# Sixteen-head attentions of a fused four-layer kernel: values and divisors from one product of 32 columns, with block transposes on VectorE and the multiplication on GpSimd

## Reference

```python
# L0 "cross": keys and values from a context of 96 features, with biases and an output projection
# L2 "masked": the same without biases and projection; masked queries attend evenly
attn = softmax(q @ k.T * 8 ** -0.5)      # per head, 128 x 128
out  = attn @ v                          # per head, 128 x 8
...
# L2 "self": causal, 16 query heads, 4 key heads; q and k rotated, then normed
out  = softmax(causal(q @ k.T / sqrt(8))) @ v
gate = sigmoid(out @ Wg + bg)
x    = x + (out * gate) @ Wo + bo
```

## Time and profile before

| | |
|---|---|
| median of 3 runs | 1946.26 us (1944.96 to 1949.05) |
| profiled execution, its own time | 1934.08 us |
| its span | 1932.3 us |
| PE busy | 1597.6 us, 83% of the span |
| DVE busy | 1342.6 us, 69% |
| ACT busy | 959.0 us, 50% |
| POOL busy | 824.1 us, 43% |
| cross phase, about | 15 to 293 us |
| masked phase, about | 800 to 1058 us |
| self phase, about | 1065 to 1415 us |

### The profile page before, as it was taken

The page is one execution under the profiler, slowest core; times in us unless marked ns, Lnnn a source line. Parts: engine busy times, 40 slices in busy tenths (PEclk is TensorE's granted clock), DMA queues, the critical chain, the costliest instruction groups (busy, mean ns, idle before and its releaser), DMA issues. The chain is left out here.

```text
span 1932.3 us, 43308 instructions
## 1 busy us (share of the span) xinstructions
PE 1597.6 (83%) x14686; PEld 1248.9 (65%) x14686; DVE 1342.6 (69%) x4056; ACT 959.0 (50%) x1953; POOL 824.1 (43%) x1300
## 2 busy tenths in 40 slices
PE   5999985977799989788997699999849699999840
PEld 3666664966577778565664466666639598888730
DVE  4878873348787777677775688888647488888522
ACT  2666662533333334366665477777725344444310
POOL 2334444346300000111111777799654555565426
PEclk9989997987799999699999699999969899999965
DMA  6657304821000000000000000000029100000043
GB/s 193 226 181 233 102 12 133 250 71 41 17 1 2 1 1 1 6 8 8 8 7 2 1 2 2 2 9 9 9 80 262 45 15 13 19 20 19 11 147 87
DMA packets 60807, 108.72 MB, mean 56 GB/s; under 512 B 11715, under 2 KB 49620, under 8 KB 59796
## 3 DMA queue, kind: packets, MB, share of 16 engines
q1 hardware_dynamic: 54452, 93.45, 15.6%
q0 software_dynamic: 6144, 12.60, 2.2%
HBM read 89.49 MB, written 52.17 MB: 73 GB/s over the span
## 5 line engine op out<-in xcount | busy, mean ns | idle before, releaser
L711 DVE TENSOR_REDUCE parts<-PS 128x8 fp32r<-128x1024 f32 x192 | 234.5, 1221 | 145.2 <-PE PS L457 145.0
L928 ACT ACTIVATE P<-PS 128x1024 f32<-128x1024 f32 x192 | 198.1, 1032 | 105.4 <-PE PS L472 105.2
L905 ACT CAST qS<-PS 32x512 fp32r<-32x512 f32 x384 | 220.8, 575 | 9.5 <-PE PS L424 6.1
L274 POOL TENSOR_TENSOR ve<-mv,eps_t 128x1 f32<-128x1 f32 x160 | 31.7, 198 | 403.9 <-DVE mv L270 403.5
L1757 DVE SCALAR_TENSOR_TENSOR X<-PS,wt,X 128x128 f32 (+1 forms) x480 | 134.9, 343 | 46.1 <-PE PS L1600 38.3
L1889 ACT ACTIVATE P<-PS,w_f_b 128x512 f32<-128x512 f32 x128 | 88.0, 687 | 142.4 <-PE PS L1581 140.9
L1600 PEld LDWEIGHTS PS<-w_f_w,P 128*128 128x128 f32 x1024 | 129.9, 193 | 39.7 <-issue 27.7
L1600 PE MATMUL PS<-w_f_w,P 128*128 128x128 f32 x1024 | 141.8, 282 | 13.6 <-DVE X L1757 11.8
L472 PE MATMUL PS<-qS,kS 128*128 128x512 f32 x384 | 151.8, 451 | 1.0 <-ACT P L928 1.0
L424 PE MATMUL PS<-ident_r,parts 128*128 128x128 f32 x768 | 124.3, 293 | 27.1 <-issue 26.2
L424 PEld LDWEIGHTS PS<-ident_r,parts 128*128 128x128 f32 x768 | 104.4, 201 | 45.7 <-issue 39.5
(11 more groups left out here) (301 smaller groups left out, 4329.6 us busy)
## 6 DMA issues: line engine op xcount, KB each, us to landing
P<-in_f_blob SPq DMA_DIRECT2D x12, 578.0 KB, 4.8
Y<-in_f_blob SPq DMA_DIRECT2D x11, 578.0 KB, 5.1
ctxT<-in_ctxT SPq DMA_DIRECT2D x128, 48.0 KB, 1.8
tok<-hs SPq DMA_DIRECT2D x46, 128.0 KB, 3.5
hs<-yo SPq DMA_DIRECT2D x46, 128.0 KB, 4.2
P<-in_f_blob SPq DMA_DIRECT2D x12, 450.0 KB, 4.4
Y<-in_f_blob SPq DMA_DIRECT2D x11, 450.0 KB, 4.5
w_f_w<-in_f_w SPq DMA_DIRECT2D x2, 1024.0 KB, 5.7
```

What stands on the lines that cost most here:

```text
L711: e.tensor_reduce(parts[:, it.s, 0, 8 * half:8 * half + 8, 3, 0], S_ps[:, :, :].rearrange("p i (j t) -> p (i j) t", t=T), AXX, ALU.max)\
L905: m = e.copy(qS[r, it.s % 2, :, j, :], TP[0][r, :].rearrange("p (g t) -> p g t", g=4))
L928: e.activation(P[:, it.s % 2, 8 * half:8 * half + 8, :].rearrange("p h t -> p (h t)"), ST_ps[:, :, :].rearrange("p j n -> p (j n)"), ACT.E ...
```

## The change

The sums come out of the product with `vx` itself. Each block of 32 columns of `vx` has 16 columns that are zero when only two heads are added up. So a call of `pe_values` is now for a pair of heads of each group: pair 0 writes values to rows 0 to 15 of each block and the sums to rows 16 and 17; pair 1 writes values to rows 16 to 31 and sums to rows 0 and 1. Columns of ones (`sum_cols`) stand in `vx` for that; `ones_x` and its 16 matmuls per item are gone. A sum is now in a row of its own, while the values that it divides are in other rows, so DVE first turns the bank `OB[:, 0:256]` in squares of 32 x 32 into SBUF (`oV`, tokens by features), takes the reciprocal of 16 sums per row, and the product `oN` is then made with a broadcast along the row, in two instructions of 64 columns: in cross and masked on POOL, in self on DVE. A second instruction of DVE, `v_heads_back`, turns `oN` back to `oT`; in cross and masked it stands at the end of DVE's tick, behind the second `v_max`.

```diff
             def pe_values(e, it, pair):
...
-                        e.wait_ge(s_o, at(s_o, it.n))
-                for j in range(4):
+                        e.wait_ge(s_tv, at(s_tv, it.n))
+                for j in (2 * pair, 2 * pair + 1):
                     for g in range(4):
...
+                        m = e.matmul(OB[32 * g:32 * g + 32, pair * T:(pair + 1) * T],
+                                     vx[:, it.s, 128 * j + 32 * g:128 * j + 32 * g + 32],
+                                     P[:, it.s % 2, 4 * g + j, :], start=(j % 2 == 0), stop=(j % 2 == 1))
...
             def v_heads(e, it):
+                e.wait_ge(s_av, at(s_av, it.n + 1))
+                if due(2 * it.n):
+                    e.wait_ge(s_on, at(s_on, 2 * it.n))
+                e.transpose(oV[:, :, :, :].rearrange("p a q r -> p (a q r)"), OB[:, 0:2 * T]).then_inc(s_tv, 1)
+                e.wait_ge(s_tv, at(s_tv, it.n + 1))
+                e.reciprocal(rec[:, :, :, :], sums).then_inc(s_rec, 1)
+                if causal:
+                    normed(e, it)
+
+            def normed(e, it):
...
+                e.wait_ge(s_rec, at(s_rec, it.n + 1))
+                for pair in range(2):
+                    own_rows = slice(16 * pair, 16 * pair + 16)
+                    e.tensor_tensor(oN[:, :, own_rows].rearrange("p q (h d) -> p q h d", h=2),
+                                    oV[:, pair, :, own_rows].rearrange("p q (h d) -> p q h d", h=2),
+                                    rec[:, pair].unsqueeze(3).broadcast_to([T, 4, 2, DH]), ALU.mult).then_inc(s_on, 1)
+
+            def v_heads_back(e, it):
...
-                e.wait_ge(s_rec, at(s_rec, it.n + 1))
-                e.tensor_tensor(oT[:, it.s, :], OB[:, 0:T], rec[:, :], ALU.mult).then_inc(s_o, 1)
+                e.wait_ge(s_on, at(s_on, 2 * it.n + 2))
+                e.transpose(oT[:, it.s, :], oN[:, :, :].rearrange("p q r -> p (q r)")).then_inc(s_o, 1)
...
                             v_residual(e, it)
                         if it := item(L):
                             v_max(e, it, 1)
+                        if it := item(L + 3):
+                            v_heads_back(e, it)
...
                     if it := item(F + 1):
                         g_low(e, it)
+                    if it := item(L + 3):
+                        normed(e, it)
```

More of the change, by code:

```diff
@@ L209, in build @@
         vx = sb("vx", [T, RING, 4 * 136])
-        ones_x = sb("ones_x", [T, 4, 4, DH])
+        sum_cols = [vx[:, :, 128 * j:128 * j + 128].rearrange("p r (g c) -> p r g c", c=32)
+                    [:, :, :, (16, 17, 0, 1)[j]:(16, 17, 0, 1)[j] + 1] for j in range(4)]
         qT = sb("qT", [D, RING, T], F32R)
@@ L475, in pe_scoresT, with pe_values @@
                 m.then_inc(s_st, 1)
-            def pe_values(e, it, what):
-                if what == 0:
+            def pe_values(e, it, pair):
+                if pair == 0:
                     issued["av"] += 1
@@ L484, in pe_values @@
                     if due(it.n):
-                        e.wait_ge(s_o, at(s_o, it.n))
-                for j in range(4):
+                        e.wait_ge(s_tv, at(s_tv, it.n))
+                for j in (2 * pair, 2 * pair + 1):
                     for g in range(4):
[L488 to L492, removed]
+                        m = e.matmul(OB[32 * g:32 * g + 32, pair * T:(pair + 1) * T],
+                                     vx[:, it.s, 128 * j + 32 * g:128 * j + 32 * g + 32],
+                                     P[:, it.s % 2, 4 * g + j, :], start=(j % 2 == 0), stop=(j % 2 == 1))
+                if pair == 1:
                     m.then_inc(s_av, 1)
@@ L871, in pool @@
                     return
-                for item in unrolled(last if post else F + 1):
+                for item in unrolled(last if post else L + 3):
                     if it := item(0):
@@ L979, in attention16 @@
                    hi=B, lo=2 * B, turn=B, kx=B, qT=B, tk=B, kS=B, tq=B, qS=B, s=2 * B, mx=2 * B,
-                   st=2 * B, exp=2 * B, av=B, rec=B, o=B, out=B, done=B, pad=n_pad)
+                   st=2 * B, exp=2 * B, av=B, rec=B, values_turned=B, values_normed=2 * B, o=B, out=B, done=B,
+                   pad=n_pad)
             if projected and not causal:
@@ L1114, in pool @@
                 e.memset(vx[:], 0.0).then_inc(sem("pad"), 1)
+                e.wait_ge(sem("pad"), at(sem("pad"), 1))
+                for j in range(4):
+                    e.memset(sum_cols[j], 1.0).then_inc(sem("pad"), 1)
                 if pre:
@@ L1151, in attention1 @@
             totals(stats=B, rstd=B, h=B, bn=B, ve=B, hps=B, hT=B, qkv=B, qk=2 * B, v=B, s=B, mx=B, nb=B,
-                   exp=B, pps=B, pT=B, av=B, rec=B, done=B, pad=1)
+                   exp=B, pps=B, pT=B, av=B, rec=B, done=B, pad=5)
             totals(**{f"ctx{i}": 16 * GROUPS for i in range(RING)})
@@ L1357, in v_heads @@
                     ob = OB[:, :].rearrange("p (h n) -> p h n", n=T)
-                    e.reciprocal(rec[:, 0:4].unsqueeze(2), ob[:, :, HD:HD + 1]).then_inc(s_rec, 1)
+                    e.reciprocal(rec8[:, :].unsqueeze(2), ob[:, :, HD:HD + 1]).then_inc(s_rec, 1)
                     if half == 0:
```

22 lines of the change are left out of this document (13 added, 9 removed).

## The result

The changed kernel took 1931.38 us in the median of 20 runs (1893.92 to 1961.69); the kernel before, on the same chips, 1941.79 (1933.79 to 1951.87). The ratio is 0.9844, interval 0.9812 to 0.9876. Over all runs the medians give 1931.38 / 1941.79 = 0.9946, and resampling the recorded runs puts that between 0.989 and 0.997. So it is faster either way, by a half to one and a half per cent. The number in microseconds is the forecast one (1931); the gain by the ratio, 1.56%, is twice the forecast 0.8%, and the one by the medians, 0.54%, less than it. And the spread is new: 68 us for 18.

A forecast was written before the change was run, and what follows sets the result against it. No engine is always busy; closed chains of engines set each tick. Masked -11.4, cross -11.6, self +5, clock +4, rest -1 sum to -15 us, taking the median from 1946.3 to 1931 us; range 1912 to 1952.

The forecast's parts named there:

- masked, mechanics: Masked: DVE's shorter heads and PE's earlier values cut the tick by 0.38 to 7.17 us; 30 ticks, -11.4 us.
- cross, mechanics: Cross: DVE's saving goes into waiting for POOL, PE turns `h` sooner; 0.40 us over 29 ticks, -11.6 us.
- self: Self: new DVE and POOL work lengthens the tick by 0.15 us over 31 ticks, +5 us.
- clock, cross and masked: Cross and masked: PE idles longer ahead of `h`, so three more drops from 2.4 to 1.2 GHz, +4 us.
- what would make it wrong: Sign against the forecast: a clock at 1.2 GHz for whole ticks.
- the clock falls twice as often: Rival, cross and masked: 14 more drops at 1.47 us, +21 for +4, 1948 us, no change; 10%.
- the chain of DVE and POOL: Self: five new instructions add 0.35 us, making this chain the longer one, 10.47 for 10.22 us.
- rival of self: Two: DVE held up beside POOL's work, +16 us, 1947, 12%; or ACT and PE set the tick, 1916, 10%.
- Unit prices: Assumed times of the new instructions: first transpose 0.45 us, transpose back 0.32, reciprocal 0.25, POOL's products 0.62 for two.
- The rival of two passes: DVE's transposes take two passes, 0.22 and 0.10 us more per item; +7 us, 1953 us, slower; 12%.

The follow-up runs named there:

- before_filled_at_scores: Kernel before with two unused 128 x 128 products ahead of the second half of the scores in cross and masked; 1930.71 us, ratio 0.9964.
- fill_behind_pair_0: Changed kernel with 8 extra matmuls per item behind pair 0 in all three phases, into columns nobody reads; 1898.34 us, ratio 0.9768.
- fill_not_in_self: Changed kernel with 8 extra matmuls behind pair 0 in cross and masked, but not in self; 1892.9 us, ratio 0.9772.
- the doubled transpose: Changed kernel with 8 extra matmuls behind pair 0 and the first transpose made twice in all phases; 1926.59 us, ratio 0.9931.
- before_filled: Kernel before with 8 more matmuls per item behind the first call of the product, into columns nobody reads; 1974.28 us, ratio 1.0197.
- fill_ahead_of_scores: Changed kernel with two unused 128 x 128 products ahead of the second half of the scores in cross and masked; 1917.55 us, ratio 0.988.
- the load back: Changed kernel with 8 unused matmuls behind each call of the value products, 32 matmuls per item as before; 1901.4 us, ratio 0.979.
- fill_product_on_vector: Changed kernel with 8 extra matmuls behind pair 0 and the product on DVE right behind the reciprocal; 1947.21 us, ratio 1.0039.

## Why the prediction was right in its number, and where it failed

Three kernels that are nearly always at 2.4 GHz in cross and masked separate the terms: before_filled_at_scores for the kernel before, fill_behind_pair_0 and fill_not_in_self for the changed one. Their ticks at 2.4 GHz are those of the unfilled kernels (7.55 and 6.97 in masked), so what the unfilled ones are longer by is the clock's.

| term, us | forecast | measured |
|---|---|---|
| masked, mechanics | -11.4 | -17 to -18 (228.9 to 210.5-211.7) |
| cross, mechanics | -11.6 | -14 to -16 (237.3 to 221.4-223.3) |
| self | +5 | +1.6 (301.6 to 303.2) |
| clock, cross and masked | +4 | +24 to +36 (below) |

- **The clock** is the step that failed: "so I allow three more drops: +4 us". The kernel before lost 245.6 + 238.0 - 237.3 - 228.9 = 17 us to it. The changed one lost 41 to 45 us in one profile (244.4 + 232.0 against 431.9 to 435.0) and 51 to 54 in the other: 24 to 36 more. These are single profiles, and that of the kernel before is of an execution near its fastest (1934.08 us, median 1941.79), so its 17 us are rather low. The runs give a check: the filled kernels differ by 0.9772 / 0.9964 = 0.981, some 37 us, and the unfilled by 10 in the medians, so the change lost some 27 us more. The form was wrong as well as the size. I read the falls of before as single events and counted more of them; in the long stretches at 2.4 GHz there are none now, and a fall, when it comes, lasts for whole ticks, which the prediction named only as what would make it wrong. The rival "the clock falls twice as often" had the right sign and neither form nor price.
- **Masked** was mis-sized: 6.97 for a forecast 7.17 and 7.55 before. Heads came to 0.63 for 0.72, maximum to `kx` to 4.01 for 4.17, `kx` to the end of `h` to 1.56 for 1.60. The rest, `h` to PE in 0.06 and PE's 1.34 to the next maximum, was as forecast.
- **Cross** too: -0.45 to -0.51 us per tick for -0.40, of which 0.05 may be the one fall that the 237.3 still hold. The transpose back waits 0.27 us in the row shown, inside the forecast 0.2 to 0.3, and 9.0 us in 26 cases on the whole. That `kx` starts hardly earlier held (3.00 for 3.10, and 3.08 before), and what is left is PE's, as reasoned.
- **Self** lost 0.05 us per tick and not 0.15. DVE waited 5 times for POOL's power, 4.5 us in all (2 times before, 3.1 us), where the prediction had it in most ticks: the chain of DVE and POOL, lengthened by 0.35 in the sum, did not become the one that sets the tick, which went from some 10.2 to 10.26 us; the doubled transpose shows that a third of such work counts. L657 ran 0.317 to 0.592 us as before, so nothing more is held up, and neither rival of self came.
- **Unit prices**: first transpose 0.42 (0.45), second 0.311 (0.32), reciprocal 0.25 (0.25), POOL's product 0.294 (0.31). The rival of two passes is excluded. The Trainium skill's 311 ns for a 128x128 transpose (VectorE: DVE Perf Modes, section "The three transpose paths") is given for bf16; the trace shows 0.311 us for fp32.
- Taken together: -15 was forecast. Mechanics of -30 to -33 (forecast -18) less 24 to 36 of clock (forecast 4) leave a few microseconds either way in one execution (-2.0 in the profiled pair) and -10 in the medians. That the median hit 1931 is luck: two errors that cancel, and a start of 1946.3 from three runs where 20 give 1941.8. The ratio of 0.9844 rests on the executions from 1893.92 to 1922.13 us, in which the clock cost less, and so shows twice the forecast gain.

What makes the change worth while in masked is mostly GpSimd's part: with the product on VectorE the tick at full clock is 7.49 us, 0.06 less than before the change. And the change can be had whole: with 8 idle matmuls behind pair 0 the kernel is at 0.977 of before, steadily.

One stretch at 1.2 GHz isn't new at all. In each of the 14 profiles the clock falls 33 to 38 us ahead of masked's first heads, in the sparse start of the phase (in the kernel before at 785.1 us, within a wait of PE for `h` of 4.37 us that ends at 786.73). What differs is how long it lasts: 30.7 us before, 68.3 and 81.9 in the two profiles of the changed kernel, 30.7 in the four that have 8 matmuls more behind pair 0 and the phase otherwise as it is, 41.0 with 4, and 85.3 with the work ahead of the scores. So the change did not make that fall; it made the return late.

What stays open: why a stretch at 1.2 GHz goes on for 40 us or ends. Not the amount of work by itself (before_filled has PE busy 42.79 of 48 us between falls and still falls, the changed kernel 112.90 of 128 and doesn't), and not idle time of PE in the slow stretch, since there is next to none once a phase runs (30.00 of 30.00 and 44.72 of 45.00 us busy). In cross the two profiles differ in where the first one starts (147.6 and 159.2 us), and it wasn't traced to an event.

## To carry to other kernels

Taking work off an engine that is not always busy can slow it: price the granted clock for both kernels, and fill a freed gap with idle matmuls where the engine waits anyway before judging the change. Find each engine's slack at the very place: the same 8 matmuls cost 0.43 us per tick ahead of `h` in one kernel and nothing in the other. When a kernel has two clock states, take several executions and compare phases tick by tick at the same clock, since one profile says little.

## What the hardware showed that I had not expected

- TensorE stayed at 1.2 GHz for 32 us with 32.00 us busy (fill_ahead_of_scores) and for 30 with 30.00 (the changed kernel). The Trainium skill (TensorE: Matmul & The Clock Gate, Part 1) ties full clock to sustained activity of the engine. By that alone these stretches would have ended long before; the measurement disagrees, and a tick of 9.70 us for 6.97 shows that the low clock is real.
- Extra work made the kernel faster and its times closer: 1900.11 to 1904.71 us with the load back, 1893.92 to 1961.69 without.
- Whether falls repeat goes neither with load nor with the tick's length alone: at 7.49 us and with the fill (fill_product_on_vector) the clock fell in every third tick, at 7.55 us (before_filled_at_scores) in none of masked's until its last ticks, and at 6.98 us with less work in none for 128 us.
